# A mixture-of-experts dispatch on one Trainium2 core: the second choice's slots in two halves, expert inputs loaded by GpSimd, one expert's weight splits and eight text-value products moved

## What is computed

```python
capacity = max(1, int(CF * N / E))
topw, topi = jax.lax.top_k(probs, K)
...
rank = jnp.arange(N * K) - starts[se]
keep = rank < capacity
pos = jnp.where(keep, rank, capacity)
disp = jnp.zeros((E, capacity + 1, D), x.dtype).at[se, pos].set(xf[st])
disp = disp[:, :capacity]
g = jnp.einsum('ecd,edf->ecf', disp, wg)
u = jnp.einsum('ecd,edf->ecf', disp, wu)
eo = jnp.einsum('ecf,efd->ecd', jax.nn.silu(g) * u, wd)
gathered = eo[se, jnp.minimum(pos, capacity - 1)]
```

## Time and profile before

| | |
|---|---|
| median of 3 runs | 1277.84 us (1275.55 to 1280.85) |
| profiled execution, its own time | 1264.48 us |
| its span in the trace | 1262.6 us |
| busy: PE | 1054.4 us (84%) |
| DVE | 663.6 us (53%) |
| ACT | 581.2 us (46%) |
| POOL | 281.5 us (22%) |
| mean granted TensorE clock | 0.901 of full speed |
| chain that ended last | PE 56%, DVE 19%, ACT 10%, DMA 5%, POOL 4%, SP's queue 3%, issue 3% |
| stage 2 in the trace | about 327 to 521 us |

### The profile page before, as it was taken

How to read it: one execution, slowest core, us unless ns; L and a number is a source line. 1 busy time by engine, 2 the same in 40 slices (tenths; PEclk the granted TensorE clock), 3 DMA queues, 4 the chain that set the end, 5 groups by cost and what they waited for, 6 DMA issues and landing times.

```text
span 1262.6 us, 20956 instructions
## 1 busy us (share of the span) xinstructions
PE 1054.4 (84%) x8288; PEld 758.4 (60%) x8288; DVE 663.6 (53%) x1646; ACT 581.2 (46%) x1368; POOL 281.5 (22%) x285
## 2 busy tenths in 40 slices
PE   7988678888784777788999878888988888778996
PEld 4677446566444777545556566666766666445654
DVE  3322455556673767345445547776676774535103
ACT  5411237545334555344444525555565564455542
POOL 2410213200150000332112110222212222232543
PEclk9876759879886999898999999999999998768998
DMA  9420225410455683354224304431332105000001
GB/s 321 92 44 1 55 64 123 129 28 11 165 175 201 217 324 123 115 164 148 85 71 139 120 33 152 125 99 34 90 98 75 50 1 208 1 1 1 1 1 30
DMA packets 66593, 123.63 MB, mean 98 GB/s; under 512 B 11536, under 2 KB 42224, under 8 KB 62416
## 3 DMA queue, kind: packets, MB, share of 16 engines
q1 hardware_dynamic: 63728, 117.48, 30.4%
q0 software_dynamic: 1536, 3.67, 0.9%
q10 hardware_dynamic: 1232, 1.15, 0.3%
HBM read 86.30 MB, written 35.92 MB: 97 GB/s over the span
## 4 chain that ended last, share of the span: by engine, by line
PE 56%; DVE 19%; ACT 10%; DMA 5%; POOL 4%; SPq 3%; issue 3%; DVEq 0%; ACTq 0%; POOLq 0%
PE psum L385 39%; ACT s_p L2469 2%; DVE s_p L2511 2%; POOL rs L2801 2%; PE psum L1205 2%; DMA values<-s_v 2%; DVE s_max L2500 2%; PE psum L2428 2%; PE psum L2439 2%; PE psum L1177 1%; PE psum L2600 1%; DVE s_pT L2492 1%; SPq L960 1%; DVE s_max L1330 1%; DVE wu L1150 1%
## 5 line engine op out<-in xcount | busy, mean ns | idle before, releaser
L2469 ACT ACTIVATE s_p<-psum,s_max 112x375 f32<-112x375 f32 x128 | 72.3, 569 | 85.9 <-DVE s_max L2500 85.9
L633 POOL TENSOR_TENSOR rstd<-meanvar,minus_half 112x1 f32<-112x1 f32 x40 | 23.3, 584 | 315.1 <-DVE meanvar L608 271.2
L1330 DVE TENSOR_REDUCE s_max<-psum 112x2 f32<-112x750 f32 x64 | 59.4, 935 | 39.3 <-PE psum L1177 38.5
L2801 POOL TENSOR_TENSOR rs<-ms,minus_half 112x32 f32<-112x32 f32 x8 | 43.5, 5442 | 110.2 <-DVE ms L2735 110.2
L385 PE MATMUL psum<-ctx,Wk 128*128 128x375 f16 x320 | 62.3, 330 | 5.0 <-ACT s_yT L2058 2.8
L385 PE MATMUL psum<-Wv,ctx 128*125 128x512 f16 x240 | 59.7, 410 | 8.0 <-issue 2.7
L2500 DVE TENSOR_REDUCE s_max<-psum 112x1 f32<-112x375 f32 x128 | 63.7, 539 | 2.1 <-PE psum L2420 2.1
L2428 PE MATMUL psum<-ident,s_p 112*125 112x112 f32 x384 | 59.6, 288 | 4.7 <-DVE s_p L2511 3.0
L1274 ACT ACTIVATE s_pT<-psum 125x672 f32<-125x672 f32 x64 | 46.7, 731 | 32.2 <-PE psum L1193 30.6
L3111 POOL TENSOR_TENSOR hidden<-raw,hidden 128x448 f16<-128x448 f32 x44 | 45.7, 1038 | 65.3 <-ACT hidden L2994 63.6
L587 ACT ACTIVATE s_v<-psum 125x512 f32<-125x512 f32 x48 | 28.5, 596 | 67.3 <-PE psum L385 47.8
(11 more groups left out here) (353 smaller groups left out, 2570.0 us busy)
## 6 DMA issues: line engine op xcount, KB each, us to landing
keys<-s_k SPq DMA_DIRECT2D x64, 187.5 KB, 2.2
s_k<-keys SPq DMA_DIRECT2D x8, 1500.0 KB, 7.4
values<-s_v SPq DMA_DIRECT2D x48, 224.0 KB
s_v<-values SPq DMA_DIRECT2D x16, 672.0 KB
raw_wg<-in_wg SPq DMA_DIRECT2D x8, 1024.0 KB, 5.8
raw_wu<-in_wu SPq DMA_DIRECT2D x8, 1024.0 KB, 5.7
raw_wd<-in_wd SPq DMA_DIRECT2D x8, 1024.0 KB, 5.3
s_kd<-k_halves SPq DMA_DIRECT2D x48, 93.8 KB, 3.9
```

The source lines that it names most:

```text
L1330: VE.tensor_reduce(s1_max[b % 2][:, 2 * p:2 * p + 2], rings["s1"][unit][0:N, :, 0:S], X, ALU.max, negate=True).then_inc(*V.up("max1", n))
L2469: SC.activation(rings["p4"][2 * n + j], rings["s4"][(n, j)][0:N, 0:S], ACT.Exp, bias=s4_max[b % 2][:, h:h + 1], accum_out=s4_sum[b % 2][:, ...
L2801: GP.tensor_tensor(rs5[b % 2][:], ms5[b % 2][:], minus_half[:], ALU.pow).then_inc(*G.up("rs5", b))
```

## The change

It has five parts, all in stage 2.

- `slot2` of the second choice is made in two halves: groups 0 to 3 get their slots, and are scattered, once they are counted; then groups 4 to 7. The first choice stays whole.
- `ein` moves from ACT's queue to POOL's.
- Expert 1's six high splits (ACT) stay ahead of the expert loop, now two at a time, each pair followed by two text-value units. Its low splits (DVE) come later: two (wg) ahead of the loop, four (wu, wd) inside expert 0 at f = 3, 4, 5, 6. In DVE's queue every low split of stage 2 waits until the last scatter has landed, which is new. `expert_in(0)` and `expert_in(1)` stand ahead of all this in the plan.
- SP's loads of expert 2's weights follow the low splits, so they too come later.
- Text values: 8 units (not 4) in the counting, after every second group; 6 (not 18) between counting and expert loop; 8 (not none) in the loop, one for each expert at f = 6. The sum is 28 as before.

```diff
+    GROUPS = ((0, 0, B), (1, 0, B // 2), (1, B // 2, B))
...
-            if b % 4 == 3:
+            if b % 2:
                 place_values(1, 2)
-        place(("slot2", k))
-        for b in range(B):
-            L_put.plan(("put", k, b))
+            for g, lo, hi in GROUPS:
+                if (g, hi) == (k, b + 1):
+                    place(("slot2", k, lo, hi))
+                    for c in range(lo, hi):
+                        L_put.plan(("put", k, c))
     place(("slots2",))
...
     def split_expert(e, j, half):
-        place(("split", e, j, half))
+        if e > 1:
+            place(("split", e, j, half))
         place(("splitlo", e, j, half))
         if half and e + 1 < E0:
             place(("load", e + 1, j))
 
+    expert_in(0)
+    expert_in(1)
     for j in range(3):
         for half in range(2):
-            place_values(3, 2)
-            split_expert(1, j, half)
-    expert_in(0)
-    expert_in(1)
+            place(("split", 1, j, half))
+        place_values(2, 2)
+    split_expert(1, 0, 0)
+    split_expert(1, 0, 1)
     place(("einT", 0))
     place(("einS", 0))
...
-            if 0 < e < E0 - 1 and f in SPLITS:
+            if e < E0 - 1 and f in SPLITS and (e or SPLITS[f][0]):
                 split_expert(e + 1, *SPLITS[f])
             if e == E0 - 1 and f == 3:
                 place(("wk4",))
+            if f == 6:
+                place_values(1, 2)
...
             elif what == "slot2":
-                k, = at
-                tab = slot_tab[:, k * B:(k + 1) * B]
+                k, lo, hi = at
+                tab, bs = slot_tab[:, k * B + lo:k * B + hi], slice(lo, hi)
                 dve.wait_ge(V.so_far())
-                VE.tensor_reduce(rank[:, k], cnt[:, k], X, ALU.add).then_inc(*V.up())
+                VE.tensor_reduce(rank[:, k, bs], cnt[:, k, bs], X, ALU.add).then_inc(*V.up())
...
             elif what == "splitlo":
+                dve.wait_ge(L_put["put", 1, B - 1])
                 vector_split(*at)
...
+            elif what == "ein":
+                e, = at
+                i = e % 2
+                pool.wait_ge(L_put["put", 1, B - 1])
+                if e >= 2:
+                    pool.wait_ge(T["einT", e - 2])
+                GP.dma_start(e_in[i][:],
+                             disp[e * CAP:(e + 1) * CAP, :].rearrange("(t p) d -> p t d", p=HC)
+                             ).then_inc(*L_in[i].up("ein", e))
```

More of the change, by code:

```diff
@@ L1770, in gpsimd_s2 @@
             elif what == "slot2":
-                k, = at
-                pool.wait_ge(V["put2", k], L_zero["zero", SLOTS // HC - 1])
-                for b in range(B):
+                k, lo, hi = at
+                pool.wait_ge(V["put2", k, lo, hi], L_zero["zero", SLOTS // HC - 1])
+                for b in range(lo, hi):
                     GP.indirect_dma_start(
```

23 lines of the change are left out of this document (7 added, 16 removed).

## The result

| | before | the change |
|---|---|---|
| median, measured side by side on one chip | 1276.55 us (20 runs) | 1269.62 us (20 runs) |
| ratio, with its 95% interval | | 0.9932 [0.9903, 0.9961] |
| profiled execution, span | 1262.6 us | 1270.2 us |
| mean granted TensorE clock | 0.901 | 0.896 |

The change is faster by 0.7% by the ratio, which is 8.7 us; the medians lie 6.9 us apart. The forecast was 1277.84 to 1267.3 us, a ratio of 0.992. The profiled execution of the change is nevertheless longer than that of before.

What follows compares the result with a forecast made beforehand. PE stood idle 14.85 us before the first expert's rows, held by ACT's queue and POOL's scatters. PE's start 13.2 us earlier, less 2.7 us in expert 0, gives -10.5 us: 1277.84 to 1267.3 us, range 1260 to 1277 us.

Steps and rivals of the forecast that it cites:

- Halves: Second choice's slots in two halves: 1.6 us more on DVE, last scatter starts at 373.7 us, 5.0 us earlier.
- Splits out of the scatters: POOL's second-choice scatters: with splits behind them the 1.25 us step holds, none takes 1.83 or 1.77 us; included in 373.7.
- Landing: From the last scatter's start to complete rows: 4.2 us, the middle of 2.6 and 5.9 us, so complete at 377.9 us.
- The rows' load: First rows loaded by POOL: 4.2 us to PE's start plus 0.9 us stall from two low splits; PE starts at 383.0 us.
- Counting with four more values: Four more text-value units in the counting: DVE's 3.2 us per two groups and six banks of lead cover them; costs nothing.
- Expert 0: Four low splits in DVE's queue in the first expert: gives back 2.6 to 2.7 us (bounds 0 and 4.5).
- One value in each expert: Expert loop: 1.09 us of PE falls ahead of its 1.55 us wait, 0.60 us on ACT is covered; costs nothing.
- the one on SP: SP's loads of expert 2 follow the low splits, in the same place of a turn as in later experts; costs nothing.
- Rival 1: Expert loop at f = 6: the eight text values land on its path, 13.5 us come back, 1280.8 us; chance 0.11.
- Rival 2: Before the first expert: ACT's six copies still wait for buffers, gain 7.9 us, 1269.9 us; chance 0.13.
- Rival 3: Counting: all four added text-value units on the path at 2.34 us, 9.4 us, 1276.7 us; chance 0.08.
- Rival 4: At the rows' load: POOL's building waits for both DVE splits, 2.3 us not 0.9 us, 1268.7 us; chance 0.08.

Runs made afterwards that it cites:

- the change again: The unaltered change run and profiled a second time against the kernel before: ratio 0.9883 [0.9836, 0.9930].
- both: The change with rows loaded by ACT, six low splits ahead of the loop released on issue, and loop values two each in experts 0 to 3: 0.9896 to before.
- values in experts 0 to 3: The change with rows loaded by ACT and the loop's eight text values placed two each in experts 0 to 3: ratio 0.9871 to before.

## Why the prediction held, step by step

The sum, -13.2 + 2.7 = -10.5 us, is what stage 2 gains in the change again: 182.54 - 172.02 = 10.52 us. The mechanism was right: the copies out of ACT's queue, the halves and the splits' wait bring PE's start forward. That the sum is met to 0.02 us is luck, for its terms were not all so good.

- **Halves.** Forecast: last scatter 34.7 us from the first counting product (373.7 - 339.0). It was 34.42 us. The kernel with whole slots has 37.85 us, but at PE's start the halves are worth 1.6 us only, because whole slots leave the landing quicker.
- **Splits out of the scatters.** I priced this at two stretched scatters, 1.8 us. That was too low for what it guards against: with the values gone, six splits cost one scatter 7.50 us, and the landing behind it took 2.7 us longer.
- **Landing.** Forecast 4.2 us; from the last scatter's start to POOL's load it was 4.57 us, and 4.63 us in the first profile. (For before the prediction took the scatters' median, 5.9 us; the last one landed in 5.1 us.)
- **The rows' load.** Forecast 4.2 us and 0.9 us of stall. Issue to PE took 2.97 us (2.84 in the first profile), with two splits beside it. POOL spent 1.48 us on two loads, and as much in the two kernels whose DVE was idle then: no stall. This is the term that I mis-sized, by 2.1 us: I took it from ACT's load of 3.94 us, which had run beside full DMA engines (a share of 0.99), and added a stall from the indirect scatters. The Trainium skill's estimate of 2.3 us ("DMA: Bandwidth & Descriptors", section "Anatomy of one DMA — SWDGE (gpsimd) path") was nearer. PE started at 41.96 us, where 44.0 was forecast.
- **Counting with four more values.** Nothing, as forecast: 27.11 us became 28.71 us, which is the added slots' 1.6 us; with the values moved and the slots whole it is still 27.11 us.
- **Expert 0.** Forecast +2.7 us; measured 14.94 - 12.93 = 2.0 us, 1.9 us in the first profile. At a like clock the splits cost what was forecast; the difference is the clock, which the prediction left out. Behind PE's start the granted clock stayed at 0.50 for 7.7 us in before, and for 5.6 and 5.9 us in the change's two profiles. With whole slots it stayed there for 7.7 us again, with the same four splits, and expert 0 took 15.68 us, 2.75 us more than before. Windows from PE's start to the first down product, before, whole slots and the change:

```profile
396.16:409.09 12.93, 11.86 (x141) 11.68 (x142) 5.12 (x15) 6.60 (x17) 0.00 (x0) 0.70 0.29 104
```

```profile
377.09:392.77 15.68, 13.08 (x145) 12.28 (x146) 9.08 (x19) 6.72 (x18) 1.32 (x2) 0.76 0.53 163
```

```profile
388.57:403.42 14.85, 12.12 (x146) 11.32 (x146) 9.04 (x19) 6.71 (x18) 1.32 (x2) 0.81 0.58 174
```

- **One value in each expert.** Nothing in five turns, as forecast; but 2.06 us in the long turn, and 0.3 us each in the last turn and behind it. The whole is 115.12 - 112.45 = 2.67 us. The step that failed is the price of a value in an expert, 1.09 us of PE and 0.60 us on ACT, "Covered: nothing", with the one on SP, "so each comes in the same place of a turn as in the later experts: nothing". I had costed PE and ACT, and not the DMAs that the values put into SP's queue ahead of the weights, and into the DMA engines beside them.

So an error of -2.1 us (the load) and -0.7 us (expert 0) met one of +2.7 us (the loop). The median's gain was 6.9 us; its interval (0.9903 to 0.9961 of 1276.55 us) is a gain of 5.0 to 12.4 us and holds the 10.5 us, as does that of the second comparison, 8.9 to 20.8 us.

Rival 1 (values on the path) came true in one turn of seven, at 1.9 to 2.1 us and through the weights. Rival 2 (ACT late) did not: ACT was free at 381.3 us in the first profile, 8.02 us before it was needed. Rival 3 (counting becomes PE's) did not. Rival 4 (DVE shuts POOL out at the load) did not at that place: loads and splits began within 0.3 us of each other, POOL's two issues took 1.48 us with the splits beside them and 1.48 us without, and the load was only 0.6 to 0.7 us slower than ACT's. Its rule (the Trainium skill, "SBUF — State Buffer", section "SBUF: two separate sides") is borne out where splits and scatters overlap, and not at these plain loads. DVE there, in the change again (POOL's issue is the row at 377.68 us above):

```profile
377.41 2.36 DVE L1150 SCALAR_TENSOR_TENSOR wg<-raw_wg,wg 128x1024 f16<-128x1024 f32 x2 [8.16 <-DMA dispatched<-x_tok,put_i]
```

Of the marks that I named as signs of being wrong, one came in both profiles, a turn over 16 us, and one in the first alone: counting the second choice took over 13.5 us (12.6 us and the 3.57 us for which DVE stood still, the added slots left out).

## What to carry to other kernels

Work that fills an idle engine can still hold a queue that the end of the wait depends on: here 18 copies, free on PE, kept ACT from the first expert's rows. When such filler is taken out, what stood between other operations closes up, and a run of DVE operations beside POOL's DMA building becomes one long lock-out; order them by a wait. Ask, too, which loads a finished split releases, and what lands beside them. And cost moved work on every queue that it enters: two DMAs a turn, ahead of a load that had 0.4 us to spare and beside it, took back 2 us of the 13 won up to the first down product.

## What the runs showed of the hardware

- DVE's run of six 1024-column operations with two SBUF inputs held one indirect DMA on POOL for 7.50 us, in two kernels, and a run of two for 2.96 us. I had expected 0.9 us for each split, as in the earlier trace rows, where the splits had gaps between them.
- A plain DMA of 140 KB issued by POOL takes it 0.65 to 0.77 us, and two splits of DVE beside it didn't lengthen that (1.48 us for two issues, with them and without). At a DMA share of 0.30 to 0.47 meanwhile PE had the rows 2.7 to 3.0 us after POOL's issue and 2.3 to 2.5 us after ACT's.
- The same load from ACT's queue took 3.94 us in before (DMA share 0.99 meanwhile), and 6.4 and 7.1 us where expert 2's weights had been issued 0.5 to 0.6 us ahead of it (0.98 and 0.96).
- In the long turn the granted clock fell to 0.50, for 3.4 or 6.8 us, in five of the six profiles in which PE's wait ahead of the next expert was 2.25 to 3.01 us. In the sixth, "both" with 2.74 us, it didn't fall, nor in the other profiles, whose wait was at most 2.12 us. In the one with 3.01 us (values in experts 0 to 3) it fell 0.8 us after the wait. What the fall costs depends on what runs in it: almost nothing in the change, 1.85 us in the two profiles where the down product fell into it.

```profile
471.42 0.53 PE L385 MATMUL psum<-e_inT,wg 128*128 128x140 f16 x6 [3.01 <-DVE e_inT L1739]
...
472.16 0.90 PE L385 MATMUL psum<-e_inT,wg 128*128 128x140 f16 x6
```

- At the first expert's start the granted clock is at 0.50 in every profile. In the eight profiles with four splits in expert 0, that expert takes the longer the longer the clock stays there: from 14.85 us with 5.6 us of it to 15.68 us with 7.7 us.
- DVE stood still for 3.57 us in one execution, with no cause in the trace and not again in nine profiles with the same counting.
